# A mixture-of-experts kernel on one core: VectorE splits h into its high and low part right behind the product that makes it

## What is computed

```
# first: 8 experts, 2 per token, inner width 256; second: 32 experts, 8 per token, inner width 192
g = silu(xt @ w_gate[e]);  u = xt @ w_up[e]
y = (g * u) @ w_down[e]
out[token] += weight[token, e] * y          # over the chosen experts of the token
x = x + out
```

## Time and profile before

| | |
|---|---|
| median of 3 executions | 1076.29 us (1075.6 to 1079.83) |
| the profiled execution | 1073.37 us, span 1071.6 us |
| TensorE matmuls busy | 811.7 us, 76% of the span |
| VectorE, ScalarE, GpSimd busy | 515.7, 524.3, 499.5 us |
| first expert loop, about 280 to 410 us | 20 tiles, 10 passes |
| second expert loop, about 604 to 1040 us | 80 tiles, 40 passes |
| mean granted TensorE clock | 0.908 of full speed |

### The profile page before, as it was taken

The page is one execution under the profiler, slowest core; times in us unless marked ns, Lnnn a source line. Parts: engine busy times, 40 slices in busy tenths (PEclk is TensorE's granted clock), DMA queues, the critical chain, the costliest instruction groups (busy, mean ns, idle before and its releaser), DMA issues.

```text
span 1071.6 us, 20434 instructions
## 1 busy us (share of the span) xinstructions
PE 811.7 (76%) x5206; PEld 441.1 (41%) x5207; DVE 515.7 (48%) x1523; ACT 524.3 (49%) x782; POOL 499.5 (47%) x413
## 2 busy tenths in 40 slices
PE   4998999997389993769871377878877778777770
PEld 3444455544244442335341243444444444444440
DVE  5653444564435533557763243544545435353432
ACT  5532334544356741345452165556756556555550
POOL 4880001001346755004575555566766556656560
PEclk9999999998589996979985698999999999989995
DMA  8553010000348958301110358878987878779668
GB/s 283 168 182 118 11 40 21 31 30 31 111 126 217 236 101 240 129 30 41 41 42 23 108 129 234 194 165 195 242 221 191 228 165 199 186 169 233 150 111 254
DMA packets 108391, 150.73 MB, mean 141 GB/s; under 512 B 18336, under 2 KB 59552, under 8 KB 108352
## 3 DMA queue, kind: packets, MB, share of 16 engines
q0 software_dynamic: 25760, 56.56, 26.9%
q1 hardware_dynamic: 80000, 93.49, 26.6%
q10 hardware_dynamic: 2592, 0.19, 0.2%
HBM read 107.34 MB, written 42.86 MB: 140 GB/s over the span
## 4 chain that ended last, share of the span: by engine, by line
PE 39%; DMA 15%; issue 14%; DVE 10%; DVEq 8%; ACT 5%; SPq 3%; POOL 3%; ACTq 2%; POOLq 0%; another core or an unknown queue 0%
PE pst L187 32%; DMA mid<-moe_normalised_rows,small 6%; DMA big<-in_L_ffn_w_down_dram 4%; DMA x_rows<-mid,small 3%; DVEq L1160 3%; DVEq L1154 2%; PE pst L1264 2%; PE pst L493 2%; POOL moe_tokens_of_experts L994 1%; DVE big L1146 1%; DMA big<-x_rows 1%; ACTq L1154 1%; DVE mid L1385 1%; DMA big<-in_L_ffn_wo_dram 1%; PE pst L953 1%
## 5 line engine op out<-in xcount | busy, mean ns | idle before, releaser
L187 PE MATMUL pst<-big,mid 128*128 (+1 forms) x1392 | 287.0, 359 | 22.1 <-DVE mid L1377 10.4
L1460 POOL DMA_INDIRECT x_rows<-mid,small x100 | 160.1, 1601 | 130.9 <-ACT mid L1321 77.0
L994 POOL DMA_INDIRECT moe_tokens_of_experts<-token_no,small x80 | 82.8, 1035 | 285.4 <-DVE small L1047 264.9
L187 PEld LDWEIGHTS pst<-big,mid 128*128 128x128 f16 x1392 | 137.8, 102 | 137.1 <-issue 47.6
L1450 POOL DMA_INDIRECT mid<-moe_normalised_rows,small x106 | 114.7, 1082 | 97.4 <-DVE small L1367 37.4
L1264 PE MATMUL pst<-big,mid 128*128 x520 | 132.3, 388 | 1.4 <-ACT mid L1313 0.9
L1302 ACT ACTIVATE mid<-pst 128x1024 f16<-128x1024 f16 x102 | 103.7, 1017 | 55.7 <-PE pst L1236 44.0
L1377 DVE SCALAR_TENSOR_TENSOR mid<-pst,small,mid 128x192 f32<-128x192 f32 (+1 forms) x100 | 42.6, 426 | 119.8 <-ACT mid L1308 87.8
L1236 PE MATMUL pst<-id,mid 128*128 128x128 f16 x816 | 66.5, 228 | 39.0 <-DMA mid<-moe_normalised_rows,small 34.5
L187 PE MATMUL pst<-ctxN,mid 128*128 128x512 f16 x384 | 88.6, 389 | 3.2 <-ACT mid L619 3.2
L1321 ACT ACTIVATE mid<-pst 128x512 f32<-128x512 f32 x100 | 59.9, 599 | 58.0 <-PE pst L1264 46.0
(11 more groups left out here) (201 smaller groups left out, 1193.4 us busy)
## 6 DMA issues: line engine op xcount, KB each, us to landing
big<-in_L_ffn_w_gate_dram SPq DMA_DIRECT2D x32, 384.0 KB
big<-in_L_ffn_w_up_dram SPq DMA_DIRECT2D x32, 384.0 KB
big<-in_L_ffn_wi_dram SPq DMA_DIRECT2D x16, 512.0 KB
big<-in_L_ffn_w_down_dram SPq DMA_DIRECT2D x32, 256.0 KB
big<-in_L_ffn_w_down_dram SPq DMA_DIRECT2D x64, 128.0 KB
moe_normalised_rows<-xn SPq DMA_DIRECT2D x18, 256.0 KB, 2.0
mid<-in_ctx_dram SPq DMA_DIRECT2D x16, 256.0 KB, 4.3
big<-in_ctx_turned_dram SPq DMA_DIRECT2D x16, 256.0 KB, 4.6
```

Source lines behind the costliest of these rows:

```text
L187: last = nc.tensor.matmul(dst, stationary(a, c), moving(b, c), start=(k == 0), stop=(k == 3 * len(parts) - 1))
L994: nc.gpsimd.indirect_dma_start(out=self.tab_d[:, :], out_offset=bass.IndirectOffsetOnAxis(ap=self.addr[j % 2][:, k:k + 1], axis=0), in_=to ...
L1460: nc.gpsimd.indirect_dma_start(out=acc_d[p][:, :], out_offset=bass.IndirectOffsetOnAxis(ap=self.si[p], axis=0), in_=self.y[p], in_offset=N ...
```

## The change

VectorE's order in the slot is altered. `h_high` and `h_low` follow `make_h` at once, with the tile and the buffer that `make_h` has just written; before, they stood in the next slot behind `weights_in_turn` and worked on the tile before. `rows_out` and the top of the next slot come behind them. The two calls behind the loop, for the last tile, are dropped. The functions themselves, all buffers and all other engines are unchanged.

```diff
@@ dve_pair
                     self.rows_in_turn(dve, it + 1 + p, t + 3, 1 - p, c[5 + p])
                     self.weights_in_turn(dve, it + 1 + p, t + 1, 1 - p, e[1 + p])
-                    if not (first and p == 0):
-                        self.h_high(dve, t - 1, 1 - p)
-                        self.h_low(dve, t - 1, 1 - p)
                     with dve.If(e[p + 1] > e[p]):
                         self.split_d_lo(dve, e[p + 1])
                     self.make_h(dve, t, p)
+                    self.h_high(dve, t, p)
+                    self.h_low(dve, t, p)
                     if not first:
                         self.rows_out(dve, it - 1, t - 2, p, c[p])
@@ dve
                 n = 2 * np_
-                self.h_high(dve, n - 1, 1)
-                self.h_low(dve, n - 1, 1)
                 c = self.columns(dve, np_, -2, 2)
```

## The result

| | before | after |
|---|---|---|
| median | 1078.06 us (1075.6 to 1081.84, 4 runs) | 1119.69 us (1114.83 to 1126.85, 4 runs) |
| ratio | | 1.0388, 95% interval 1.0321 to 1.0456 |
| profiled span | 1071.6 us | 1116.5 us |
| first loop, first to last make_h | 95.8 us (301.4 to 397.2) | 107.3 us (298.7 to 406.0) |
| second loop, first to last make_h | 421.9 us (615.8 to 1037.7) | 454.9 us (628.4 to 1083.4) |

In the changed kernel L1447 is the gather and L1457 the scatter (L1450 and L1460 before); the lines of VectorE quoted here kept their numbers.

The account below looks back on a forecast made before the run. The loops were taken as bound by waits, in two rings of nearly one length, through silu and through the gather. +24.6 - 14.7 - 5.0 - 0.2 = +4.7, plus 1, about +6 us on 1076.29: 1082 us, range 1071 to 1097.

Parts of the forecast that it names:

- the likeliest case: Over both loops, an exchange with a small loss: 1078 to 1088 us, chance 0.45.
- the high part meets POOL at another place: VectorE's cast (L1385) beside GpSimd's split: sum -4 us (1072) or +13 (1090), left at nothing; no chance of its own.
- 8.5 us: Excess time of all 80 L1385 casts in the kernel before: 26.9 us against 0.23 us each alone.
- POOL's scatters (behind L1372) can come later: GpSimd's scatters wait for rows_out, which now stands behind the four instructions; noted, with no size given.
- The 0.88 us: Added between make_h and rows_out, charged at 28 visits of the chain to rows_out or the loads: +24.6 us.
- The sum along the chain (+4.7 us): VectorE's visits on the old chain through both loops: +24.6 added, -19.9 saved; the kernel can't end before this.
- 1 us on top: Estimate for the gather ring's 0.1 us and for passes with a p = 1 split, where VectorE was late.
- the prediction's sign: Median time from L1361 at the top to the next: unchanged or 0.1 to 0.2 us longer.
- 0.70: Saved ahead of VectorE's split (L1141), 1.13 - 0.43 us, at 21 visits of the chain: -14.7 us.
- 5.2: Saved ahead of turning h, 5 visits at 1.0 us each (-5.0), and 0.2 us at one more.
- It moves to L1236: TensorE's wait at L1252 becomes waiting for gathered rows: 2.5 us instead of 1.55 at the p = 1 tile.
- The clock rival: TensorE's longer waits lower its clock in 10 more passes: +16 us, 1098; chance 0.18, shared with a longer ring.

Follow-up runs that it names:

- run 3: Kernel before, with GpSimd's split (L1134) cut to 8 of 384 columns in the second mixture: ratio 1.0014, second loop 425.7 us.
- run 9: Kernel before, with only the even tile's high and low part at once on make_h, but behind rows_out: ratio 1.0023 to before, second loop 420.4 us.
- run 5: Changed kernel with GpSimd's split cut to 8 of 384 columns in the second mixture, plus 26 semaphore increments on GpSimd: ratio 1.0243 to before, second loop 434.4 us.
- run 7: Changed kernel with rows_out moved ahead of h_high and h_low, right behind make_h: ratio 1.0149 to the kernel before, second loop 435.6 us.
- run 4: Changed kernel with GpSimd's split (L1134) cut to 8 of 384 columns in the second mixture: ratio 1.0208 to the kernel before, second loop 430.3 us.
- run 8: Changed kernel with 24 added matmuls keeping TensorE busy behind the p = 0 down product: ratio 1.0359 to the kernel before, second loop 454.8 us.
- run 10: Changed kernel with rows_out ahead of h_high and h_low, and GpSimd's split cut to 8 of 384 columns: ratio 0.9990 to before, second loop 419.2 us.
- run 12: Changed kernel with GpSimd's even-tile scatter issued behind the p = 1 gather: ratio 1.0517 to the kernel before, second loop 467.5 us.
- run 6: Changed kernel with GpSimd's split (L1134) moved behind the scatter of its slot, all work kept: ratio 1.0373 to the kernel before, second loop 448.9 us.

## Why the prediction was wrong

It forecast 1082 us in a range of 1071 to 1097 and gave 0.42 to slower. The direction of the likeliest case was right, the size off by a factor of seven (6 us against 42), outside the range. Two steps failed, the first two below, and they act together. By its steps:

- **"I leave it at nothing" was the step that failed** (the high part meets POOL at another place). The rival was named and bounded at +13 us, by doubling 8.5 us of stretching. Both halves of the bound were wrong. First, its size: only the casts were thought to be stretched, but L1394, with two tensor inputs, took 2.41 us, and the parts took 22.6 us more in the second loop, not 8.5 more. Second, its price: stretching isn't worth its own length. Run 3 shows that the 8.5 us before cost nothing measurable, in run 9 casts of 450 ns in the mean cost 0.2%, and in the changed kernel 20.5 us of the second loop hang on it (run 5): nothing in one place, nearly its own length in another. By runs 7 and 9 what counts is what stands behind the stretched instruction: before, VectorE's split and the turning of h; after, `rows_out`, L1361 and L1367. This step alone doesn't account for the miss: with nothing stretched in the second loop, runs 4 and 5 still stand at 1.021 and 1.024, which on 1076.29 us is 1099 and 1102 us, above the range. The Trainium skill (GPSIMD Engine Reference, Specifications) says that the SBUF interfaces shared with VectorE give contention both with two-port modes and with two SBUF inputs. The row at 941.44 agrees; the section that the prediction named covers the first case alone.
- **"POOL's scatters (behind L1372) can come later"** was written down and given no price. The 0.88 us were charged only where the chain of before went on from make_h to the loads. No chain of before went from `rows_out` to the scatter, so it got a cost of nothing. Run 9 shows that the even tile's 22.8 us hang on the place ahead of `rows_out`, and run 7 that with `rows_out` first the whole is at 1.015, about 1092 us and inside the range, though the parts are stretched as in the changed kernel.
- **The sum along the chain (+4.7 us)** was called a floor for the new time, and then used as the forecast with 1 us on top. Its terms hold roughly, but they were read along the old chain, and 33.0 us over 40 passes are 0.8 us a pass, where the prediction's sign was 0.2 at most. These are VectorE's rows in a slot with a split in the changed kernel:

```profile
916.90 0.15 DVE L1367 COPY small<-mid 128x1 f32 x1
917.55 0.96 DVE L1141 TENSOR_TENSOR big<-big  x1 [0.49 <-issue]
...
919.63 0.40 DVE L1377 SCALAR_TENSOR_TENSOR mid<-pst,small,mid 128x192 f32<-128x192 f32 x1
...
920.86 0.15 DVE L1372 COPY small<-big 128x1 int32 x1
```

  From L1377 to L1372 it is 1.23 us (1.22 forecast), from L1367 to L1141 0.65, not 0.43; both are also the medians of the second loop. So the queue's own work was no longer hidden at all: a split gains 1.13 - 0.65 = 0.48 and not 0.70, and the sum would be 24.6 - 21 x 0.48 - 5.2 = +9.3 us. With nothing stretched the second loop lost 4.6 us (run 4 against run 3), or 12.5 with GpSimd's time kept (run 5 against before).
- **"It moves to L1236"** (TensorE's wait) held in part: 44.7 to 4.4 us at L1252, 29.0 to 61.5 us at L1236. But 29.3 us more came up at the gate-up, which waits for make_h (8.2 to 37.5), a place that the prediction didn't name. That the 44.7 us don't come back held.
- **The clock rival** was right as an observation, the granted clock in the second loop fell to 0.89, and the 4.05 us gate-up behind 4.17 us of waiting is its row. As a cause of the loss runs 8 and 10 speak against it. The Trainium skill (TensorE: Matmul & The Clock Gate, HAM oscillation) describes this throttling behind waits for DMA; no run here shows it to be worth a measurable time.

What stays open: the share of the scatter against the gather behind it (run 12), the place of the 16.4 us between runs 7 and 10, and the first loop. Of its 11.5 us the odd half of the change alone costs 5.3 and the even half 9.6; with `rows_out` first it takes 102.1 (run 7) and 103.0 us (run 10), so about half of the loss went, and the rest has no cause shown.

## What to carry to other kernels

Before an instruction is moved forward on an engine, price each message that it now stands ahead of, also those that aren't on the chain of waits today: a floor worked out along the old chain says nothing of the new one. A stretched instruction is cheap or dear by what is queued behind it, so sending the message first (`rows_out`, then the work for h) was worth 19 us of the second loop here and took no work away. It made the change less bad and not good: run 7 is still 1.5% slower than before. And a wait that an engine loses is a gain only if its next wait is not in the same ring.

## What the runs showed of the hardware that I had not expected

- A VectorE subtraction with two SBUF inputs (L1394) was held until GpSimd's split ended, 2.41 us instead of 0.29, although it had begun 0.60 us before it by the profile, whose times for GpSimd are rough. It happened seven times in the second loop, each beginning 0.5 to 0.6 us ahead and ending 0.16 us behind the split. Casts of 128x128 from f32 to f16 behaved alike (up to 1.62 us instead of 0.23); those above 0.9 us all began behind the start of the split and ended 0.1 us behind its end.
- Both engines can be slowed: with the splits of both engines side by side (run 6) L1146 took 2050 ns instead of 736 and L1134 2198 instead of 1646.
